# Third cast of a tile's bytes in the counting stage: from ScalarE to GpSimd

## What is computed

```python
def step(h, _):
    messages = h[col] @ W_msg.T + b_msg
    agg = segment_sum(messages, row, num_segments=3125)
    gi, gh = agg @ W_ih.T + b_ih, h @ W_hh.T + b_hh
    r, z = sigmoid(i_r + h_r), sigmoid(i_z + h_z)
    n = tanh(i_n + r * h_n)
    return (1.0 - z) * n + z * h
h = scan(step, x, length=5)
out = layernorm(x + h)
```

## Time and profile before

| | |
|---|---|
| median of 3 runs | 647.53 us (645.96 to 648.52) |
| profiled execution | 646.73 us, of which span 644.9 us |
| TensorE busy | 604.8 us (94%) |
| VectorE busy | 333.5 us (52%) |
| ScalarE busy | 319.6 us (50%) |
| GpSimd busy | 288.6 us (45%) |
| mean granted TensorE clock | 0.978 |

### The profile page before, as it was taken

How to read it: one execution, slowest core, us unless ns; L and a number is a source line. 1 busy time by engine, 2 the same in 40 slices (tenths; PEclk the granted TensorE clock), 3 DMA queues, 4 the chain that set the end, 5 groups by cost and what they waited for, 6 DMA issues and landing times.

```text
span 644.9 us, 8625 instructions
## 1 busy us (share of the span) xinstructions
PE 604.8 (94%) x3071; PEld 472.2 (73%) x3071; DVE 333.5 (52%) x729; ACT 319.6 (50%) x557; POOL 288.6 (45%) x399
## 2 busy tenths in 40 slices
PE   4579999999999999999999999999999999999991
PEld 4467777778557788777877778877788877888850
DVE  3799999986576222246322224712333552343356
ACT  3569888884445443345433344534443444343342
POOL 6112222220303666643665655466666455666500
PEclk9589999999999999999999999999999999999996
DMA  6024566553000000000000000000000000000012
GB/s 168 25 77 123 120 119 120 123 120 41 1 1 2 1 0 1 0 1 0 2 1 1 1 0 1 0 1 1 0 2 0 2 1 0 1 0 1 1 41 62
DMA packets 32107, 18.68 MB, mean 29 GB/s; under 512 B 4588, under 2 KB 31082, under 8 KB 32062
## 3 DMA queue, kind: packets, MB, share of 16 engines
q1 hardware_dynamic: 28104, 13.32, 9.6%
q0 software_dynamic: 2016, 4.22, 2.5%
q10 hardware_dynamic: 1942, 0.55, 0.4%
HBM read 2.96 MB, written 1.60 MB: 7 GB/s over the span
## 4 chain that ended last, share of the span: by engine, by line
PE 79%; DMA 7%; DVE 5%; ACT 4%; issue 2%; SPq 1%; POOL 0%; DVEq 0%
PE PS L708 42%; PE PS L688 8%; PE PS L689 8%; PE PS L631 6%; DMA A<-stage 5%; PE PS L696 4%; PE PS L695 4%; PE PS L551 4%; PE PS L622 2%; ACT spread L882 2%; SPq L444 1%; ACT ring L928 1%; DVE hot_row L1178 1%; ACT stage L870 1%; DMA row_of<-in_dst,small 1%
## 5 line engine op out<-in xcount | busy, mean ns | idle before, releaser
L515 POOL CAST ring<-A 128x896 fp32r<-128x896 uint8 (+4 forms) x324 | 250.2, 809 | 214.9 <-PE PS L708 200.0
L708 PE MATMUL PS<-ring,parts 128*128 128x448 f32 x1372 | 302.9, 375 | 1.9 <-ACT ring L928 1.9
L708 PEld LDWEIGHTS PS<-ring,parts 128*128 128x128 f32 x1372 | 254.5, 188 | 32.5 <-issue 11.7
L1213 DVE SCALAR_TENSOR_TENSOR pre_n<-PS,small,gate_r 128x448 f32<-128x448 f32 x35 | 23.9, 684 | 232.7 <-PE PS L696 232.7
L928 ACT ACTIVATE ring<-A 128x896 fp32r<-128x896 uint8 (+4 forms) x144 | 106.1, 776 | 0.1
L911 ACT ACTIVATE gate_r<-PS,small 128x448 f32<-128x448 f32 x35 | 22.2, 633 | 154.7 <-PE PS L689 154.7
L631 PE MATMUL PS<-spread,parts 128*128 128x448 f32 x294 | 83.2, 394 | 3.3 <-ACT spread L882 3.2
L882 ACT ACTIVATE spread<-A 128x1056 fp32r<-128x1056 uint8 (+1 forms) x75 | 70.8, 949 | 10.1 <-DMA A<-stage 9.9
L506 POOL DMA_DIRECT2D A<-stage x50 | 26.6, 532 | 103.0 <-ACT stage L870 103.0
L688 PE MATMUL PS<-hT,wT 128*128 128x448 f32 x140 | 64.4, 542 | 0.6 <-ACT agg L904 0.6
L622 PE MATMUL PS<-hot_row,hot_key 128*128 128x132 bf16 x588 | 56.0, 232 | 6.6 <-DVE hot_row L1178 6.5
(11 more groups left out here) (125 smaller groups left out, 491.5 us busy)
## 6 DMA issues: line engine op xcount, KB each, us to landing
A<-stage SPq DMA_DIRECT2D x150, 66.0 KB, 3.2
A<-stage POOLq DMA_DIRECT2D x50, 66.0 KB, 3.0
y<-in_x SPq DMA_DIRECT2D x4, 384.0 KB, 4.9
out<-y SPq DMA_DIRECT2D x4, 192.0 KB, 2.2
out<-y SPq DMA_DIRECT2D x3, 256.0 KB, 2.2
w_raw<-in_L_gnn_W_ih ACTq DMA_DIRECT2D x1, 192.0 KB, 4.0
w_raw<-in_L_gnn_W_hh ACTq DMA_DIRECT2D x1, 192.0 KB, 5.7
w_raw<-in_L_gnn_W_msg ACTq DMA_DIRECT2D x1, 64.0 KB, 2.0
```

What stands on the lines that cost most here:

```text
L515: last = nc.gpsimd.tensor_copy(to, data)
L708: mm = pe.matmul(PS[:, AGG_BANKS[(t * LEGS + b) % 2], 0:LW], parts[:, k, part, :], ring[:, SLOT_OF[at_piece] % SLOTS, k % 2, :], start=(k ...
```

## The change

The third cast of each tile (576 columns, byte 2) leaves ScalarE's program and comes into GpSimd's, as `spread_last_byte(k)`. It stands there behind GpSimd's DMA issue of pair 4k+8 (for the last two tiles behind the loop), with the same waits: the tile has landed, the buffer is used up. It signals a semaphore of its own, `spread_by_pool`, and `wide` waits for that before the items j = 4 and 5. ScalarE makes two casts per tile, behind the pairs 4k+7 and 4k+8. Nothing else differs. Of the 25 casts 23 lie in the loop.

```diff
--- before.py
+++ after.py
@@ -283,6 +283,7 @@
         hots_ready, counted, count_kept = sem("hots_ready"), sem("counted"), sem("count_kept")
         stored = [sem("stored0"), sem("stored1")]
         stored_too = [sem("stored_too0"), sem("stored_too1")]
+        spread_by_pool = sem("spread_by_pool")
         spread_made, spread_used, late_made, late_used = (
             sem(n) for n in ("spread_made", "spread_used", "late_made", "late_used"))
         first_made, kept_by_act, kept_by_dve = (sem(n) for n in ("first_made", "kept_by_act", "kept_by_dve"))
@@ -347,11 +348,13 @@
         def items_until(p):
             return max(0, p - USE_AT) * (LEGS - 1) // PT
 
-        CASTS = tuple((k, i) for k in range(KT) for i in range(len(SPREADS)))
+
+        BY_ACT_TOO = len(SPREADS) - 1
+        CASTS = tuple((k, i) for k in range(KT) for i in range(BY_ACT_TOO))
 
         def casts_until(p):
             k, n = divmod(max(0, p - SPREAD_AT), PT)
-            return len(SPREADS) * k + min(n, len(SPREADS))
+            return BY_ACT_TOO * k + min(n, BY_ACT_TOO)
 
 
         EARLY = 8
@@ -500,10 +503,22 @@
             pool.wait_ge(flag_set, 1)
             fast = pool.value_load(flag, min_val=0, max_val=1)
             with pool.If(fast == 1):
+                def spread_last_byte(k):
+                    a, w, z, lo = SPREADS[-1]
+                    pool.wait_ge(stored[k % 2], landed(k))
+                    pool.wait_ge(stored_too[k % 2], landed_too(k))
+                    if k >= 2:
+                        pool.wait_ge(spread_used, (LEGS - 1) * (k - 1))
+                    nc.gpsimd.tensor_copy(spread[:, k % 2, lo:lo + z - w], A_bytes[:, k, w:z, a]).then_inc(spread_by_pool, 1)
+
                 for p in range(PAIRS):
                     if p % PT in STORED_TOO:
                         pool.wait_ge(count_kept, p + 1)
                         nc.gpsimd.dma_start(*placing(p, 1)).then_inc(stored_too[p // PT % 2], 16)
+                    if p >= SPREAD_AT + 1 and (p - SPREAD_AT - 1) % PT == 0:
+                        spread_last_byte((p - SPREAD_AT - 1) // PT)
+                for k in range((PAIRS - SPREAD_AT - 2) // PT + 1, KT):
+                    spread_last_byte(k)
 
                 pool.wait_ge(first_made, LEGS)
                 for at_piece in SEQUENCE:
@@ -637,7 +652,9 @@
                         pe.wait_ge(parts_ready, k // 2 + 1)
                     if (k, MSG_BANKS_FIRST[0]) == (0, j):
                         pe.wait_ge(msg32_ready, UNITS)
-                    pe.wait_ge(spread_made, k * len(SPREADS) + SPREAD_FOR[j])
+                    pe.wait_ge(spread_made, k * BY_ACT_TOO + min(SPREAD_FOR[j], BY_ACT_TOO))
+                    if SPREAD_FOR[j] > BY_ACT_TOO:
+                        pe.wait_ge(spread_by_pool, k + 1)
                     return both_parts(k, j, spread[:, k % 2, j * LW:(j + 1) * LW])
 
                 def last_leg(k):
```

## The result

The changed kernel takes **675.85 us** (median of 6 runs, 672.2 to 678.93), the one before 647.41 us (6 runs, 645.96 to 648.56): ratio 1.0436, 95% interval 1.0411 to 1.0462. That is 28 us slower, where 6.5 were forecast, and outside the range. The direction was right, the size was not.

The account below looks back on a forecast made before the run. VectorE (4.21 us a tile) and TensorE (4.26) bound the counting, later a transfer loop (4.54). Cast costs to VectorE of +3.8, +1.4, +0.5, +0.5 and +0.3 made +6.5 us: 653.2, as median 654.0; range 649.5 to 659.

Parts of the forecast that it names:

- What bounds the kernel: Counting stage: VectorE at 4.21 and TensorE at 4.26 us per tile; in the second half a transfer loop at 4.54.
- ScalarE's term: 25 casts of 0.69 us leave ScalarE in the counting stage; claimed worth nothing while VectorE is the slowest.
- GpSimd's own time: GpSimd's cast with its wait for VectorE done in 1.1 to 1.3 us, about 3.3 us of cover: costs nothing.
- VectorE's term: Each GpSimd cast holds up VectorE's counting by 0.48 us (bounds 0.35, 0.67), giving 4.69 us per tile; +6.5 us in all.
- The clock: TensorE's clock in the counting stage should hold at 2.4 GHz, with TensorE busy about 91% instead of 94%.
- the cast comes late: VectorE's row never lets GpSimd's cast in until VectorE stands at `counted`; 5.2 us a tile, +16 us, 664; chance 0.06.
- TensorE waits for the cast of GpSimd: Sign against the prediction in the changed profile: TensorE waiting for the moved cast; no size given.
- The groups keep their means: Sign against the prediction: VectorE's hot_key and hot_row groups not longer than 559 and 504 ns on the mean.
- Tiles of 4.21 us: Sign against the prediction: tiles early in the counting loop still taking 4.21 us, where 4.7 was expected.

Follow-up runs that it names:

- The run that only writes: The changed kernel with GpSimd filling the 576 columns with a constant in place of casting the bytes, so it reads nothing from SBUF: 649.31 us.
- the run that always admits the cast: The changed kernel with VectorE waiting for GpSimd's cast of tile k before it begins pair 4k+11: 659.64 us.

## Why the prediction was wrong

- **What bounds the kernel**: right. VectorE and TensorE at 4.21 and 4.26 us a tile, ScalarE behind. The run that only writes has ScalarE relieved and shows no gain.
- **ScalarE's term, nothing**: right as far as the same run tells (+1.4 us, with the fill in GpSimd's queue).
- **GpSimd's own time**: here the prediction failed. It put "the cast with its wait for VectorE" at 1.1 to 1.3 us, since the earlier trace rows show a cast wait for one instruction of VectorE, and found cover enough in the three pairs until TensorE needs the bytes. Measured: 8 of 25 casts stay out while VectorE's row goes on, seven of them until it stops, up to 5.9 us, and TensorE stands seven times for them, 21.5 us in all. The rows it rested on were of another kind: L1220, L1225 and L1229 each wait for the result of the one ahead, so there is a gap behind each, and the casts shown found one. The prediction saw that difference ("the instructions of the counting have none") and used it to set the price; that the cast might not get in at all it left to the rival at 6%.
- **VectorE's term**: right mechanism, undersized. 0.48 us was taken, 0.74 to 0.76 measured; it lay outside the bounds of 0.35 to 0.67. The columns were right (0.24 us for 288), the fixed 0.28 us was missing. In the earlier trace rows VectorE's instruction came 0.04 us behind the start of the cast's record; in the counting it begins 0.20 us ahead of it and stands all the same. Where the 0.28 us come from the records don't tell; the rows of the steps don't hold them. With 0.72, VectorE's rise in the run that always admits the cast (4.93 for 4.21), the prediction's own sum gives 8 x 0.72 + 12 x (4.93 - 4.57) + 0.7 + 0.7 + 0.5 = 12 us, so 659.5: that run measured 659.64 (its four longer tiles are not in the sum, so the nearness is partly luck). The sum is sound where its premise, that every cast gets in, is made true.
- **The clock**: wrong. It was expected to hold at 91% busy; it did in the runs without such stands (0.976 to 0.981), but behind six of the seven stands of TensorE it fell to 1.2 GHz (behind the first and shortest, 2.82 us, it stayed at 1.00). TensorE's 12.3 us of extra busy time is about what this can have taken. How the loss (30.9 us in the profiled execution) divides between standing (21.5 us of waits for the cast) and the clock wasn't tried apart; their sum is over the loss, since part of either is hidden.
- **The rival "the cast comes late"** named the mechanism that came true, at 6%, and priced it at 664: it charged 0.9 us a tile for the cast and a short gap and left out that TensorE stands while VectorE works off its lead of three buffers, and that the clock falls behind. It also took every cast to be kept out, and only some are.
- **What would show it**: the text named three signs against itself. "TensorE waits for the cast of GpSimd" came, in 7 waits. "The groups keep their means" came too: hot_key at 554 ns and hot_row at 500, no more than in the earlier trace rows; this sign is a weak one, since the casts that got in fell mostly on hot_high. Tiles of 4.21 us came in part, in one tile of three, the one in which the cast is kept out.

## To carry to other kernels

Before work goes to GpSimd, look at how VectorE's instructions follow each other there. Where they read two tensors of SBUF and leave no gap, as here, a GpSimd instruction that reads SBUF was either paid in full by VectorE (0.74 us for one of 0.67) or not done at all for several us, and whatever stood behind it in GpSimd's queue was late as well. A mean price per instruction from a stretch with gaps didn't hold in one without. If the work must be there, give it its place in VectorE's program (here 16 us better than leaving it to chance), or let GpSimd do what only writes.

## What the runs showed that was not expected

- A reading GpSimd instruction was kept out for some 10 us by instructions that each ended after 0.3 to 0.6 us (its record is 10.6 us long, in one case 11.0). The Trainium skill's page SBUF — State Buffer (section Who interferes with whom) says that whoever issues first holds the shared ports for the whole instruction and the other blocks. The admitted casts agree (0.74 us for VectorE); for the row of VectorE instructions the runs show more than that: the cast didn't get its turn between two of them, 26 times over.
- Whether a cast got into the unbroken row hung on a tenth of a microsecond: at 0.11 to 0.25 us behind the start of a VectorE instruction 40 of 42 got in, at other moments 4 of 38.
- A GpSimd fill at the same place, which only writes, was never kept out (0.60 us at most in all 25). The same section of the Trainium skill's page says that a VectorE instruction with two SBUF inputs contends with a GpSimd instruction that reads SBUF and not with one that only writes it; the 0.60 us agree, for bf16 too.
- Fewer buffers made a kernel faster, by 20 us (675.85 to 655.91 us): VectorE's row then had a late start of 0.08 us or more in most tiles, and there the casts got in.
